# First cross-attention of a two-layer perceiver on one core: the order of the steps on all engines

## What is computed

```
xn = layernorm(ctx)            # 32 batches x 257 rows x 384
ln = layernorm(x)              # 32 batches x 32 latents x 512
q  = ln @ Wq.T                 # 8 heads of 64
kv = concat([xn @ Wkv.T, ln @ Wlkv.T])     # 257 + 32 = 289 keys
qn = rmsnorm(q) * qn_g * 64**-0.5
kn = rmsnorm(k) * kn_g
attn = softmax(qn @ kn.T + mask)           # per head
out  = attn @ v
```

## Time and profile before

| what | us |
|---|---|
| median of 3 runs | 1886.89 (1886.12 to 1889.93) |
| the profiled execution's own time | 1886.4 |
| its span, first to last instruction | 1884.7 |
| busy PE, PE weight loads, DVE, ACT, POOL | 1602.9, 1134.3, 1285.4, 992.8, 682.7 |
| busy PE, DVE, ACT, POOL in 153.3 to 540 us, inside `cross0` (386.7 us) | 350.5, 326.0, 270.8, 260.0 |

### The profile page before, as it was taken

How to read it: one execution, slowest core, us unless ns; L and a number is a source line. 1 busy time by engine, 2 the same in 40 slices (tenths; PEclk the granted TensorE clock), 3 DMA queues, 4 the chain that set the end, 5 groups by cost and what they waited for, 6 DMA issues and landing times. The chain is left out here.

```text
span 1884.7 us, 43587 instructions
## 1 busy us (share of the span) xinstructions
PE 1602.9 (85%) x16191; PEld 1134.3 (60%) x16191; DVE 1285.4 (68%) x2885; ACT 992.8 (53%) x2210; POOL 682.7 (36%) x795
## 2 busy tenths in 40 slices
PE   6958899999976788659999999769996299989996
PEld 3525566666654566547777777525553278778775
DVE  7858888888854677548888888567776754444441
ACT  5646777777743344336666666433332465555541
POOL 4556676676621111011111111125553123323332
PEclk9979999999996899779999999889998599999998
DMA  5121011111102000021111111431000665565512
GB/s 198 43 72 35 26 44 35 43 38 38 34 24 108 1 2 2 1 67 34 34 34 34 34 34 34 161 115 30 13 13 12 221 197 152 156 182 158 137 30 69
DMA packets 50105, 126.95 MB, mean 67 GB/s; under 512 B 6913, under 2 KB 19553, under 8 KB 49889
## 3 DMA queue, kind: packets, MB, share of 16 engines
q1 hardware_dynamic: 44914, 112.64, 18.5%
q0 software_dynamic: 5008, 11.80, 3.2%
HBM read 110.83 MB, written 15.68 MB: 67 GB/s over the span
## 5 line engine op out<-in xcount | busy, mean ns | idle before, releaser
L106 PE MATMUL e_pGU<-XT,WB 128*128 128x128 f16 x1344 | 232.7, 222 | 18.7 <-issue 8.8
L107 PE MATMUL e_pGU<-XT,WB 128*128 128x128 f16 x1344 | 232.5, 222 | 0.6 <-issue 0.6
L108 PE MATMUL e_pGU<-XT,WB 128*128 128x128 f16 x1344 | 232.5, 222 | 0.0
L2640 DVE SCALAR_TENSOR_TENSOR WB<-w5in,WB 128x1024 f16<-128x1024 f32 x96 | 115.5, 1223 | 85.9 <-ACT WB L2782 85.9
L106 PEld LDWEIGHTS e_pGU<-XT,WB 128*128 128x128 f16 x1344 | 133.8, 100 | 23.9 <-issue 22.4
L107 PEld LDWEIGHTS e_pGU<-XT,WB 128*128 128x128 f16 x1344 | 133.8, 100 | 1.5
L108 PEld LDWEIGHTS e_pGU<-XT,WB 128*128 128x128 f16 x1344 | 133.8, 100 | 0.8 <-issue 0.8
L106 PE MATMUL dpK<-dLT,W 128*128 128x256 f16 x384 | 106.0, 276 | 18.7 <-POOL dLT L1741 18.7
L2623 POOL TENSOR_TENSOR XT<-e_mf,XT 128x256 f16<-128x256 f32 x84 | 56.2, 669 | 173.4 <-ACT XT L2796 173.4
L1752 POOL TENSOR_TENSOR XT<-dzo,XT 128x128 f32 (+1 forms) x32 | 13.7, 427 | 283.9 <-ACT XT L1897 283.9
L734 POOL TENSOR_TENSOR crn<-css,mhalf 128x8 f32<-128x8 f32 x64 | 106.4, 1663 | 5.3
(11 more groups left out here) (556 smaller groups left out, 5746.5 us busy)
## 6 DMA issues: line engine op xcount, KB each, us to landing
w5in<-in_WE SPq DMA_DIRECT2D x96, 512.0 KB, 5.1
cx<-in_ctx SPq DMA_DIRECT2D x32, 384.0 KB, 3.3
dx<-in_ctxT SPq DMA_DIRECT2D x32, 384.0 KB
w5in<-in_W SPq DMA_DIRECT2D x14, 512.0 KB, 8.5
wpiece<-in_W SPq DMA_DIRECT2D x12, 512.0 KB, 9.8
w3in<-in_W SPq DMA_DIRECT2D x11, 512.0 KB, 4.7
cv<-vlat SPq DMA_DIRECT2D x32, 96.0 KB
X<-in_x SPq DMA_DIRECT2D x8, 256.0 KB, 8.6
```

The source lines that it names most:

```text
L106: pe.matmul(out, lh, rh, start=first, stop=False, skip_group_check=shared)
L107: pe.matmul(out, lh, rl, start=False, stop=False, skip_group_check=shared)
L108: return pe.matmul(out, ll, rh, start=False, stop=last, skip_group_check=shared)
L2640: dve.scalar_tensor_tensor(WB[w][:, 1, a], ring[n][:, :], WS, WB[w][:, 0, a], ALU.mult, ALU.subtract)\
```

## The change

- The orders of all four engines' loops change, as the diff shows. `norm` moves from the end of a step to the start of the next; on PE, `outputs` and `mix(.,1)` move likewise from the end to the start, which leaves their place in the sequence as it was, and `turn_key(.,0)` moves behind `turn_context`; on DVE, `out_low` goes ahead of `mix_low(.,1)`, `tail_low` behind `mix_low(.,0)`; on ACT, `context_high` goes near the end and `rows_high` near the start; on POOL, `power` and `rows_low` go ahead of `rms(.,0)`, and `gather_keys` behind `context_low`.
- The maximum is negated by the reduction itself, and its scaling instruction goes. The factor 64**-0.5 moves into the key norm (`HD0` in the scale of the squares), so that the exponential has scale 1.
- `stats` does both halves side by side instead of one after the other.
- `turn_probs` waits for two scalings, and the scaling and turning of the tail (`tail_scale`, `turn_tails`) get places and semaphores of their own.
- In `outputs`, the `minus` operand gets 99 rows instead of 2 (97 of zeros), and its two matmuls come after both of `base`.

```diff
-                pool.tensor_scalar(ss[i][:, :], ss[i][:, :], 1.0 / (HD0 * WS * WS), 1e-16, ALU.mult, ALU.max)
+                pool.tensor_scalar(ss[i][:, :], ss[i][:, :], HD0 / (HD0 * WS * WS), 1e-16 * HD0, ALU.mult, ALU.max)
...
             for s in STEPS:            # POOL
+                if on(s + 1):
+                    power(s + 1)
                 if on(s - 1):
+                    rows_low(s - 1)
                     rms(s - 1, 0)
-                    gather_keys(s - 1)
                 if on(s):
                     context_low(s)
-                    rows_low(s)
-                if on(s + 2):
-                    power(s + 2)
+                    gather_keys(s)
                 if on(s - 1):
                     rms(s - 1, 1)
...
                 for i in range(2):
-                    ln.stats(dve, i, 2 * b + i, cx[u][:, i, :])
+                    dve.bn_stats(bn[i][:, :], cx[u][:, i, :]).then_inc(sig["c0_stat"], 1)
+                for i in range(2):
+                    dve.wait_ge(sig["c0_stat"], 6 * b + 1 + i)
+                    dve.bn_aggr(mv[i][:, 0:2], bn[i][:, :]).then_inc(sig["c0_stat"], 1)
+                for i in range(2):
+                    dve.wait_ge(sig["c0_stat"], 6 * b + 3 + i)
+                    dve.tensor_scalar(mv[i][:, 2:3], mv[i][:, 1:2], EPS, None, ALU.add).then_inc(sig["c0_stat"], 1)
...
-                dve.tensor_reduce(mx[:, :], pS[:, :, 0:KEYS], AX.X, ALU.max).then_inc(sig["c0_mx"], 1)
-                dve.wait_ge(sig["c0_mx"], b + 1)
-                dve.tensor_scalar(nm[:, :], mx[:, :], -SCALE, None, ALU.mult).then_inc(sig["c0_nm"], 1)
+                dve.tensor_reduce(nm[:, :], pS[:, :, 0:KEYS], AX.X, ALU.max, negate=True).then_inc(sig["c0_nm"], 1)
...
             for s in STEPS:            # DVE
+                if on(s + 1):
+                    norm(s + 1)
                 if on(s - 7):
                     out_low(s - 7)
+                if on(s - 3):
+                    mix_low(s - 3, 1)
+                if on(s - 1):
+                    key_scale(s - 1, 0)
                 if on(s - 2):
                     softmax_max(s - 2)
...
                     squares(s - 1, 1)
+                if on(s - 2):
+                    tail_scale(s - 2)
+                if on(s - 1):
                     key_low(s - 1, 0)
                 if on(s - 2):
                     probs_low(s - 2)
-                    tail_low(s - 2)
...
                 if on(s - 2):
                     mix_low(s - 2, 0)
+                    tail_low(s - 2)
                 if on(s - 1):
                     key_low(s - 1, 1)
-                if on(s + 2):
-                    norm(s + 2)
-                if on(s - 2):
-                    mix_low(s - 2, 1)
-                if on(s):
-                    key_scale(s, 0)
...
             for s in STEPS:            # ACT, new order in full
                 gather(s-1) exps(s-2) square(s-1,1) rows_high(s+1) key_high(s-1,0) probs_high(s-2)
                 affine(s+1) square(s,0) mix_high(s-2,0) tail_high(s-2) key_high(s-1,1)
                 out_high(s-6) context_high(s+1) mix_high(s-2,1)
...
             def turn_probs(b):
-                pe.wait_ge(sig["c0_pr"], 4 * b + 4)
+                pe.wait_ge(sig["c0_pr"], 2 * b + 2)
...
                     pe.matmul(strip(j), base[:, cols], PTt[:, slots, g, qs], start=False, stop=False, skip_group_check=True)
-                    pe.matmul(strip(j), base[0:2, cols], minus[:, :], start=False, stop=False, skip_group_check=True)
+                for j in range(2):
+                    h = 2 * c4 + j
+                    pe.matmul(strip(j), base[:, h * HD0:(h + 1) * HD0], minus[:, :], start=False, stop=False, skip_group_check=True)
...
             for s in STEPS:            # PE, new order in full
                 outputs(s-7) mix(s-3,1) scores(s-2) keys(s-1,1,0..2) turn_context(s+1) turn_key(s-1,0)
                 keys(s,0,0) turn_probs(s-2) keys(s,0,1) turn_tails(s-2) keys(s,0,2) mix(s-2,0) turn_key(s-1,1)
```

More of the change, by code:

```diff
@@ L316, in rms_power @@
                 a, r = ss[i][0:rows, :], rn[i][0:rows, :]
-                pool.tensor_scalar(a, a, 1.0 / (HD0 * WS * WS), 1e-16, ALU.mult, ALU.max).then_inc(sig[f"ms{i}"], 1)
+                up = HD0 if i else 1.0
+                pool.tensor_scalar(a, a, up / (HD0 * WS * WS), 1e-16 * up, ALU.mult, ALU.max).then_inc(sig[f"ms{i}"], 1)
                 pool.wait_ge(sig[f"ms{i}"], n + 1)
@@ L624, in cross0 @@
     W = st["W12"][:, :, :].rearrange("p a (k n) -> p a k n", k=XK)
-    SCALE = HD0 ** -0.5
     QUAD, RING, HG = 4, 8, H0 // 2
@@ L636, in cross0 @@
         pr = sb(c, "probs", [P, 2, KEYS])
-        mx, nm, rsum, rinv = (sb(c, n, [P, 2]) for n in ("cmx", "cnm", "crsum", "crinv"))
+        nm, rsum, rinv = (sb(c, n, [P, 2]) for n in ("cnm", "crsum", "crinv"))
         PT = sb(c, "cPT", [P, 2, 2, 2, P], F16)
@@ L658, in cross0 @@
         block = c.enter_context(nc.Block())
-        ln = Norm(sig, "c0", st["work"])
+        (st0, mv0, rs0), (st1, mv1, rs1) = st["work"]
+        bn, mv, rs = (st0, st1), (mv0, mv1), (rs0, rs1)
         maskrow = st["maskrow"]
@@ L713, in _ @@
                 pool.memset(qbd[u][:, :, :, :], 0.0).then_inc(sig["c0_const"], 1)
-            pool.memset(minus[:, :], -WS).then_inc(sig["c0_const"], 1)
+            pool.memset(minus[:, :], 0.0).then_inc(sig["c0_const"], 1)
+            pool.wait_ge(sig["c0_const"], 4)
+            pool.memset(minus[0:2, :], -WS).then_inc(sig["c0_const"], 1)
             def power(b):
                 for i in range(2):
-                    ln.power(pool, i, 2 * b + i, mhalf)
+                    pool.wait_ge(sig["c0_stat"], 6 * b + 5 + i)
+                    pool.tensor_tensor(rs[i][:, :], mv[i][:, 2:3], mhalf[:, 0:1], ALU.pow).then_inc(sig["c0_rstd"], 1)
             def context_low(b):
@@ L768, in norm @@
                 for i in range(2):
-                    ln.scale(dve, i, 2 * b + i, cx[u][:, i, :], y[u][:, i, :])
+                    dve.wait_ge(sig["c0_rstd"], 2 * b + 1 + i)
+                    dve.tensor_scalar(y[u][:, i, :], cx[u][:, i, :], mv[i][:, 0:1], rs[i][:, 0:1], ALU.subtract, ALU.mult)\
+                       .then_inc(sig["c0_norm"], 1)
             def squares(b, i):
@@ L939, in exps @@
                 for g in range(2):
-                    act.activation(pr[:, g, :], pS[:, g, 0:KEYS], ACT.Exp, bias=nm[:, g:g + 1], scale=SCALE,
+                    act.activation(pr[:, g, :], pS[:, g, 0:KEYS], ACT.Exp, bias=nm[:, g:g + 1], scale=1.0,
                                    accum_out=rsum[:, g:g + 1]).then_inc(sig["c0_exp"], 1)
@@ L949, in tail_high @@
                     act.wait_ge(sig["c0_q"], CK * ((b - RING) // QUAD) + CK)
+                act.wait_ge(sig["c0_tt"], b + 1)
                 act.activation(PTt[:, b % RING, :, :], turned, ACT.Copy).then_inc(sig["c0_ptthi"], 1)
@@ L990, in _ @@
                 if on(s + 1):
-                    affine(s + 1)
+                    rows_high(s + 1)
+                if on(s - 1):
+                    key_high(s - 1, 0)
                 if on(s - 2):
                     probs_high(s - 2)
-                    tail_high(s - 2)
+                if on(s + 1):
+                    affine(s + 1)
                 if on(s):
                     square(s, 0)
+                if on(s - 2):
+                    mix_high(s - 2, 0)
+                    tail_high(s - 2)
+                if on(s - 1):
+                    key_high(s - 1, 1)
+                if on(s - 6):
+                    out_high(s - 6)
                 if on(s + 1):
                     context_high(s + 1)
-                if on(s - 2):
-                    mix_high(s - 2, 0)
-                if on(s - 1):
-                    key_high(s - 1, 1)
-                if on(s + 1):
-                    rows_high(s + 1)
                 if on(s - 2):
@@ L1071, in turn_probs, with turn_tails @@
                     for i in range(2):
-                        pe.transpose(pP[:, (2 * g + i) * P:(2 * g + i + 1) * P], pr[:, g, i * P:(i + 1) * P], ident[:, :])
+                        t = pe.transpose(pP[:, (2 * g + i) * P:(2 * g + i + 1) * P], pr[:, g, i * P:(i + 1) * P], ident[:, :])
+                t.then_inc(sig["c0_pt"], 1)
+            def turn_tails(b):
+                pe.wait_ge(sig["c0_thrice"], 2 * b + 2)
+                for g in range(2):
                     t = pe.transpose(pS[0:TAIL, g, D - P:D], thrice[:, g, :], ident[:, :])
-                t.then_inc(sig["c0_pt"], 1)
+                t.then_inc(sig["c0_tt"], 1)
             def mix(b, g):
@@ L1127, in _ @@
             for s in STEPS:
+                if on(s - 7):
+                    outputs(s - 7)
+                if on(s - 3):
+                    mix(s - 3, 1)
                 if on(s - 2):
@@ L1130, in _ @@
                 if on(s - 1):
-                    turn_key(s - 1, 0)
                     for k in range(XK):
@@ L1135, in _ @@
                     turn_context(s + 1)
+                if on(s - 1):
```

(8 more changed lines are left out.)

12 lines of the change are left out of this document (5 added, 7 removed).

## The result

The changed kernel takes 1815.58 us (median of 4 runs, 1813.99 to 1816.03) against 1886.86 (4 runs, 1886.12 to 1889.93) measured beside it: a ratio of 0.962 with a 95% interval of 0.9603 to 0.9637. The profiled execution has a span of 1814.3 where the old one had 1884.7, 70.4 less.

What follows compares the result with a forecast made beforehand. A loop through several engines bounded the kernel, PE's issue time afterwards; 22 steady steps at 1.80 (-39.6), ramp -8, last three -4, drain -5, start -1, transfers +1.5 summed to -56.1: 1830.8 us, range 1820 to 1858.

Steps and rivals of the forecast that it cites:

- The bound: Steady step of `cross0`: PE's own issue time decides, 11.37 us instead of 13.15, with the gap at the turning gone.
- The negated maximum: On DVE, removing L795 takes 0.6 us off the way to the probabilities; the negating reduction still takes 0.76.
- The statistics: On DVE, both halves side by side take 1.45 us instead of 1.96, saving 0.5.
- The tail apart: Tail scaling, 0.54 us on DVE, hides behind PE's key matmuls; PE's 1.06 us gap at the turning goes wholly.
- The outputs: Four matmuls of L1111 and L1112 on PE take 0.13 us in all instead of 0.66, saving 0.5 a step.
- rival A: Matmuls of L1111 and L1112 keep their 0.165 us each; step 11.86, time 1848. Chance 0.12.
- The loop through POOL: New loop of DVE and POOL in the steady step sums to 11.1 us, 0.3 under PE's, and holds nothing up.
- rival B: The new loop through POOL decides the step, priced at 12.3 us; time 1857. Chance 0.17.
- C: Slower: POOL's powers take 1.66 us instead of 0.55 beside DVE's norm and scalings; step 13.8, time 1905. Chance 0.04.
- The transfers: Context transfers behind outputs on the SP queue: longer waits for five batches cost 1.5 us, between 0 and 4.
- The ramp and the start: First six steps: -8 us (bounds -4 and -10); start, where statistics and maximum lie bare: -1.
- Behind the last scores: End of the stage: shorter `cthrice` wait, no `out_low` wait, four outputs 0.7 less each: -5 us (bounds -2 and -6).

Runs made afterwards that it cites:

- e4: New orders of all engines alone; maximum's scaling, statistics one after the other, tail and 2-row outputs as in the kernel before: 1864.84 us, ratio 0.9883.
- e6: e5 with POOL's old order as well: 1843.06 us, ratio 0.9751.
- e8: Kernel before, the maximum negated by a second reduction over one element instead of a multiplication: 1879.81 us, ratio 0.9943.
- e5: Kernel after, with the maximum and its scaling by minus one as separate instructions again: 1819.77 us, ratio 0.9639.
- e7: Kernel before, statistics written out without the helper, which drops one separate semaphore increment: 1881.07 us, ratio 0.9961.
- e3: Kernel before, old orders and outputs, with the negated maximum, statistics side by side and tail apart: 1850.42 us, ratio 0.9811.
- e1: Kernel after, with `minus` in `outputs` back to 2 rows and its matmuls alternating with `base`: 1835.56 us, ratio 0.9715.
- e2: Kernel after, keeping 99 rows in `minus` but with `base` and `minus` matmuls alternating: 1815.73 us, ratio 0.9611.
- e11: Kernel after, the mask's matmul over 128 rows, 127 of them zero: 1814.67 us, ratio 0.9609.
- e9: Kernel after, each `power` on POOL done twice, the first into a tile nobody reads: 1836.85 us, ratio 0.9732.
- e10: Kernel after, POOL's `rows_low` moved behind `gather_keys`: 1820.19 us, ratio 0.9639.
- e12: Kernel after with the edits of e10 and e11 together: 1817.82 us, ratio 0.9633.

## Why the prediction was right in kind and short in size

**The bound.** Right. PE's own issue is the new bound, busy PE is 100% of the stretch, and no gap names `cthrice`. The size was 11.37 and came out 11.09. The step that failed is "PE carries the loop with 13.15 - 1.06 - 0.28 = 11.81 us of its own issue": some 0.2 of that was not its own. In the kernel before, the 18 matmuls of `mix(.,0)` take 351.46 to 352.57, 1.11 us, and 1.01 after. This 0.10 is a wait without a bracket in the rows: `turn_key(.,1)` at 352.57 comes 0.06 behind the end of `key_scale` on DVE (351.82 + 0.69), and in the kernel after `key_scale` ends 0.29 ahead. Turning probabilities and tails takes 0.71 and now 0.44 + 0.22 = 0.66, as the first two transposes behind the stop of 1.06 take 0.05 more. The two key turnings take 0.48 and 0.58, now 0.44 and 0.54; why is open. The last part isn't PE's issue of before but the saving: the outputs take 1.42 and now 0.85, 0.57 less where the forecast had 0.5. Together 0.30, where the step is 0.28 shorter than forecast. Over 22 steps that is 6 us, of the 7 that the middle gave beyond its terms.

**The negated maximum.** The 0.6 is right as a sum and wrong as a price. The instruction costs 0.17 to 0.21; 0.43 was a wait for POOL's `rows_low`, and the new orders alone take it away (e4; with POOL's old order it is back in e6, and a reduction doesn't have it, e8). In the new kernel, putting the instruction back costs 0.21 a step (e5) and by the medians some 4 us, which the intervals don't tell apart from nothing; without the longer power on POOL that came with it, it would have cost some 0.02 a step.

**The statistics.** Forecast 1.45, measured 1.34. "An instruction that waits for the one before it starts 0.14 after its end" is the failed sentence: it starts 0.03 to 0.04 after (e7), and the rest was the increment. In the new kernel the aggregation waits for the first half's statistics, which are long done, and starts 0.08 ahead of the end of the second's (300.67 + 1.01 to 301.60). The Trainium skill ("VectorE: DVE Perf Modes", The DRAIN you can't avoid) says that chaining with a semaphore costs nothing. It is nearer to e7 than my reading. Still, an instruction that doesn't wait starts about 0.08 ahead of the end of the one before, and side by side the statistics take 1.34 where e4 needs 310.39 - 308.64 = 1.75; so the rule doesn't hold to the last tenth here.

**The tail apart.** Right as far as it shows: PE turns the tails 0.22 us long between two key matmuls and has no gap there. It wasn't tried alone; together with the negated maximum and the statistics it gives 13.15 - 11.98 = 1.17 us in the old order (e3). What it gives by itself is not shown.

**The outputs.** Right, 0.12 for the forecast 0.13, and rival A is out (e1, e2). The Trainium skill ("TensorEngine Tiling (Array Packing)", Key Properties) has the drain at a change of tiling mode; e1 and e2 agree with it and give it a size, 0.165 instead of 0.03 for each matmul. The one row of the mask (e11) shows the same, smaller: 0.10 ahead of the pair and 0.09 in it.

**The loop through POOL (rival B).** It didn't decide. The forecast had it at 11.1, 0.3 under PE's 11.37. e5, e9 and e11 put it at 10.87, 10.88 and 10.86, and its terms read from the kernel after sum to 10.9 (the two powers are 1.03 there, not 1.2, and the statistics 1.34, not 1.45). That is 0.2 under PE's 11.09, so both were overstated by about as much, and that the distance came out nearly right is luck. C is out in this kernel: the statistics' powers kept 0.54 beside DVE's work. But its mechanism exists in small: the reason given against it, that POOL's instructions keep their durations beside DVE's, doesn't hold for the second key norm's power in e4, e5 and e11, 1.85 for 1.67.

**The transfers.** Forecast +1.5, measured under 1: one step of 11.89 in the middle, from the maximum at 277.20 to that at 289.09, with DVE waiting 0.73 for `cx`; the one behind it takes 0.18 of that back.

**The ramp and the start.** -12.4 for -8, and -3.1 for -1 (the first transfer is issued at 108.18 instead of 106.40, so from there it is -4.9). The failed step is that the middle's saving was used for a stretch that another thing bounds. In the ramp's second step PE had waited 3.4 us for `cthrice`; it now waits 1.4 for the probabilities, 2.0 less, not 1.3. And `rows_low`'s place, which I had taken as neutral, is worth 2 to 3 us in the ramp and something at the start (e10, e12). The granted clock in the first two steps was 0.93 and 0.88 before (windows of the kernel before from one maximum to the next):

```profile
143.64:158.77 15.13, 14.24 (x106) 9.09 (x104) 13.63 (x29) 11.02 (x24) 9.44 (x10) 0.93 0.14 44
158.77:172.88 14.11, 9.77 (x76) 6.49 (x75) 11.47 (x27) 8.81 (x22) 7.75 (x10) 0.88 0.07 18
```

It is 1.00 in both steps after. By the busy PE that can be 1.0 us and 1.2 us at most (7% of 14.24 and 12% of 9.77); how much of it lay on the path wasn't tried.

**Behind the last scores.** -8.3 for -5. The failed term is "four outputs at 0.7 less each, at the lower clock there". They are 1.39 less each. The windows of one such output in the kernel before, and of two and a half in the kernel after:

```profile
565.75:568.79 3.04, 2.29 (x31) 1.70 (x32) 0.29 (x1) 0.28 (x1) 0.00 (x0) 0.50 1.02 419
```

```profile
500.11:504.30 4.19, 2.71 (x90) 2.52 (x90) 0.58 (x2) 0.56 (x2) 0.00 (x0) 1.00 1.03 416
```

and PE's timeline of the kernel after there:

```profile
500.11 0.69 PE L1128 MATMUL cpO<-w3in,cWg 128*64 128x128 f16 x18 [0.75 <-issue]
500.61 0.25 PE L1133 MATMUL cpO<-cPTt,cbase 99*64 99x128 f16 x2
...
500.72 0.30 PE L1141 MATMUL cpO<-cPTt,cv 99*64 99x32 f16 x8
```

An output follows the one before in 1.66 us instead of 3.05. Of the 1.39, 0.86 are the four matmuls (0.97 to 0.11), 0.43 the eighteen (0.93 to 0.50), the rest the last eight. The eighteen are the same instructions in both; they run at the lower level of 1.2 GHz in the kernel before and at 2.4 GHz after. e1, which differs from the kernel after in the two rows alone, has the lower level and 3.05 again (its row at 518.93, with 0.93 for the eighteen). e4, though, has the two rows too and runs its first two loose outputs at a granted clock of 1.00: there one follows the other in 2.21. So of the 1.39, 2.21 - 1.66 = 0.55 are the rows at the upper level, and 3.05 - 2.21 = 0.84 the level of the clock. For the rows at the lower level the forecast of 0.7 was about right: in the output before these, which the kernel after runs at that level, the four matmuls take 495.82 to 496.04, 0.22 for 0.97. That the level would change was in no term. Counted either way it is worth 0.6 to 0.8 in each of the four outputs, about 3 of the 8.3 us, and that much is luck.

Four times 1.39 are 5.6. The other 2.7 lie between the last maximum and the first loose output, 13.14 us before and 10.42 after: 0.64 as far as the turning (the wait on `cthrice`, forecast 0.6), 0.89 from there to `mix(.,0)`, 0.47 in the output between the two mixes, and 0.72 behind that. In this last piece the wait of 1.57 on `out_low` is gone, but `mix(.,1)` runs at the lower level and takes some 0.9 more.

**The chances.** Faster was given 0.93. The range was too narrow at its lower end: each bound was worked out from a row, but none allowed for the main term, PE's own issue, being wrong, though it carries 22 steps, nor for another level of the clock behind the last scores.

## What to carry to other kernels

Before a duration is used as the price of an instruction, see what the other engines do at its end: if an instruction of POOL ends at the same hundredth in step after step, the price is a wait, and it moves with POOL's order. What an engine "issues" before a change is an upper bound for what it will need after it, since short waits show no releaser; take it from the matmul counts and the spacing where nothing is waited for. When three loops stand within 0.2 us of each other, as here after the change, savings of 0.2 bring little (e11, e12). And an edit moves every later instruction: in e5 and e11 it brought POOL's power behind DVE's norm and so lengthened another engine's work by 0.18, which has to be looked for before the difference is put down to the edit.

## What the runs showed of the hardware that was not expected

- **A small scaling on DVE waits for POOL's whole instruction.** 128x2 numbers took 0.17 us with POOL idle (the first batches), 0.60 and 1.08 when POOL was in an elementwise instruction between SBUF tiles, ending each time 0.01 to 0.04 behind that one; the same numbers through a reduction took 0.15 beside it (e4, e6, e8). The prediction had looked at POOL's side alone, whose durations stay in the rows it gave. The Trainium skill ("SBUF — State Buffer", Who interferes with whom) says that `tensor_scalar` can take a port pair that DVE shares with GpSimd, that the other side is then blocked and not slowed, and that a reduction never contends on this chip; the three kernels agree. The scalings of the probabilities, which have a scalar from a tile, kept their duration beside POOL: no run here was made to show why.
- **POOL's instructions can be longer beside DVE, too.** The power of 128x8 numbers took 1.85 instead of 1.67 us where it started 0.13 to 0.15 behind DVE's norm (e4, e5, e11, in nearly every middle step), 1.67 where it started 0.18 ahead (kernel after, e2), and 1.68 where it started 0.32 behind (e9). The cause wasn't tried.
- **An increment of a semaphore as an instruction of its own costs 0.1 us on DVE** (e7).
- **Two rows among 99 cost 0.135 us for each matmul** at 2.4 GHz (0.165 against 0.03), and 0.24 against 0.05 (0.93 for eighteen) at 1.2 GHz. With the clock it goes together only in part. In the stage's last outputs the granted clock was 0.50 in the kernel before, e1, e3, e7 and e8, all with two rows, and 1.00 or near it in the kernel after, e2, e5, e6 and e9 to e12, all with equal rows. But e4, with two rows, had 1.00 in the first two and 0.56 in the third. What sets the level here stays open.
